# Row sums in the last column of the normalised operand, sweep 5's support step behind the next row's combination, x by blocks on SP's queue

## What is computed

```python
# layer 0
u = tanh([x, t] @ W1 + b1) @ W2 + b2
x = layernorm(x + u + adj @ (x @ B.T) - sum(adj, axis=1) * (x @ B.T))
# layer 1 (Chebyshev, three products with adj)
T1 = adj @ x; T2 = 2 * (adj @ T1) - x; T3 = 2 * (adj @ T2) - T1
x = layernorm(x + x @ w0 + T1 @ w1 + T2 @ w2 + T3 @ w3 + bias)
# layer 2
h = (adj @ x + x) / clip(sum(adj, axis=1) + 1, 1)
z = relu([x, h] @ W + b); x = layernorm(x + z / max(norm(z), 1e-12))
# layer 3
support = x @ weight
w = 0.5 ** (number of later nonzeros of the row), the last 100 only
x = layernorm(x + (adj != 0) * w @ support + bias)
```

## Time and profile before

| | |
|---|---|
| median of 3 runs | 3405.94 us (3402.93 to 3409.38) |
| the profiled execution, its own time | 3407.66 us |
| its span, first to last instruction | 3405.7 us |
| mean granted TensorE clock | 0.962 of full speed |
| PE busy | 3226.4 us (95%) |
| DVE busy | 3068.7 us (90%) |
| ACT busy | 2328.3 us (68%) |
| moved by DMA | 1150.26 MB, 338 GB/s |

### The profile page before, as it was taken

One profiled execution on the slowest core, in us unless ns is written; L12 is line 12 of the kernel. 1 busy time (PEld: TensorE's weight loads), 2 busy tenths in 40 slices (PEclk: granted clock), 3 DMA queues, 4 the chain that ended last, 5 costly groups with the idle time before them and its releaser, 6 DMA issues.

```text
span 3405.7 us, 37111 instructions
## 1 busy us (share of the span) xinstructions
PE 3226.4 (95%) x14316; PEld 2388.4 (70%) x14316; DVE 3068.7 (90%) x2614; ACT 2328.3 (68%) x1561; POOL 16.3 (0%) x39
## 2 busy tenths in 40 slices
PE   6999899999989999999998999988989999999998
PEld 5877677777767888778886788766767555555554
DVE  6778888999999988999889999988899899999997
ACT  4666456555467766877777766755566688888886
POOL 1000000000000000000000000000000000000000
PEclk9999999999999999999999999978888999999999
DMA  9888577677679999999999999967789999999996
GB/s 334 316 309 312 210 286 294 245 275 270 243 286 370 398 374 377 390 390 387 378 377 374 360 376 370 383 258 286 289 347 354 371 363 384 384 387 386 387 387 241
DMA packets 159837, 1150.26 MB, mean 338 GB/s; under 512 B 17968, under 2 KB 18160, under 8 KB 20336
## 3 DMA queue, kind: packets, MB, share of 16 engines
q1 hardware_dynamic: 156672, 1140.92, 86.5%
q0 software_dynamic: 544, 2.66, 0.4%
q10 hardware_dynamic: 2448, 4.33, 0.4%
HBM read 1145.74 MB, written 2.10 MB: 337 GB/s over the span
## 4 chain that ended last, share of the span: by engine, by line
PE 66%; DVE 27%; DMA 3%; issue 2%; ACT 2%; ACTq 0%; DVEq 0%
PE ACC L801 25%; DVE lo L562 16%; PE ACC L817 14%; PE ACC L926 13%; DVE GS L556 4%; PE PSF L940 3%; PE PST L940 3%; DMA raw<-in_at 2%; ACT hi L399 1%; PE PSF L890 1%; PE PSF L891 1%; PE PSF L883 1%; DVE SV L668 1%; PE PST L831 1%; PE PST L857 1%
## 5 line engine op out<-in xcount | busy, mean ns | idle before, releaser
L399 ACT CAST hi<-raw 128x2048 fp32r<-128x2048 f32 x832 | 1586.0, 1913 | 828.1 <-PE ACC L801 610.9
L562 DVE TENSOR_TENSOR lo<-raw,hi 128x2048 fp32r<-128x2048 f32 x832 | 1883.3, 2288 | 182.7 <-ACT hi L399 175.6
L801 PE MATMUL ACC<-hi,T 128*128 128x512 f32 x5568 | 1447.2, 398 | 33.5 <-POOL T L388 11.0
L801 PEld LDWEIGHTS ACC<-hi,T 128*128 128x128 f32 x5568 | 1060.2, 192 | 279.4 <-issue 45.8
L817 PE MATMUL ACC<-lo,T 128*128 128x512 f32 x3200 | 892.1, 401 | 100.9 <-DVE lo L562 99.6
L817 PEld LDWEIGHTS ACC<-lo,T 128*128 128x128 f32 x3200 | 606.9, 192 | 270.2 <-DVE lo L562 144.9
L405 ACT ACTIVATE Wf<-ACC,w_bias 128x1024 fp32r<-128x1024 f32 x512 | 569.2, 1115 | 138.3 <-PE ACC L926 138.1
L577 DVE SCALAR_TENSOR_TENSOR M<-raw,M 128x512 bf16<-128x512 f32 x1008 | 629.7, 685 | 36.3 <-PE ACC L926 23.7
L926 PE MATMUL ACC<-M,rank_b 128*128 128x512 bf16 x2032 | 528.9, 382 | 5.8 <-DVE M L577 2.1
L926 PEld LDWEIGHTS ACC<-M,rank_b 128*128 128x128 bf16 x2032 | 159.1, 98 | 264.2 <-issue 126.4
L940 PE MATMUL PST<-Wf,S 128*128 128x512 f32 x512 | 209.6, 490 | 0.0
(11 more groups left out here) (142 smaller groups left out, 1247.5 us busy)
## 6 DMA issues: line engine op xcount, KB each, us to landing
raw<-in_at SPq DMA_DIRECT2D x1088, 1024.0 KB, 6.0
O<-in_x_rows ACTq DMA_DIRECT2D x8, 256.0 KB, 35.7
SV<-in_x_cols POOLq DMA_DIRECT2D x1, 2048.0 KB, 27.9
out<-O ACTq DMA_DIRECT2D x8, 256.0 KB, 2.4
bias<-in_bias_rows ACTq DMA_DIRECT2D x1, 128.0 KB, 10.8
l1w_sb<-in_l_w POOLq DMA_DIRECT2D x2, 64.0 KB, 8.1
rank_f<-in_rank_mats POOLq DMA_DIRECT2D x1, 128.0 KB, 10.0
w_sb<-in_w POOLq DMA_DIRECT2D x2, 64.0 KB, 11.5
```

What stands on the lines that cost most here:

```text
L399: nc.scalar.copy(hi[:, c % NH], raw[:, c % NR]).then_inc(hi_done, 1)
L562: tt(lo[:, c % NR], raw[:, c % NR], hi[:, c % NH].bitcast(f32), ALU.subtract).then_inc(lo_done, 1)
L801: ins = mm(acc[:, part], w, hi[:, p.c % NH, s, part], start=opens and s == 0 and i == 0, stop=False)
```

## The change

Three things are changed.

1. **Row sums.** `write_v` leaves the last of the 64 columns of the normalised operand out (63 are written), so that column keeps the ones with which POOL filled it. A row of a layer norm sums to zero, so the missing column is minus the sum of the others, and the matrix `drop`, multiplied once at the start into `comb2` (`mix` on PE, `mixed` on DVE), puts it back where product 2 is used; where the operand itself is needed (`whole`, k = 3) it is kept in `RS`. `GS`, its adds, the matmuls with ones and `flush` are gone; `ut` takes all 128 partitions of both groups and adds them, and the accumulators alternate from group to group in sweep 1 as they do in the others.
2. **Sweep 5.** `l3w` is due behind pair c + 16 instead of c + 14, `s_hi` behind c + 20 instead of c + 17, `s_lo` behind c + 19 instead of c + 17. Layer 2's bias goes in as a 65th row of `comb`'s operands `TX` and `l2w_sb` instead of an add on DVE (line 632).
3. **x.** The blocks of x and `bias` are issued by SP, block b ahead of tile 4b, instead of by ACT all at the start.

The core of the diff:

```diff
-            if k == 1:
-                acc_of[k, kind, r] = 0 if kind == "P" or r == 0 else 1
-            else:
-                acc_of[k, kind, r] = turn % 2
-                turn += 1
+            acc_of[k, kind, r] = turn % 2
+            turn += 1
...
+    due("PE", 12, "mix", 1, 0)
+    due("DVE", 16, "mixed", 1, 0)
...
-            due("PE", c + 14, "l3w", k, r)
-            due("ACT", c + 17, "s_hi", k, r)
-            due("DVE", c + 17, "s_lo", k, r)
+            due("PE", c + 16, "l3w", k, r)
+            due("ACT", c + 20, "s_hi", k, r)
+            due("DVE", c + 19, "s_lo", k, r)
...
             for c in range(n_all):
+                if c < NB * NP and c % NP == 0:
+                    g = gs(pairs[c].J)
+                    sp.dma_start(O[:, g], x_rows[:, g]).then_inc(c_x[c // NP], 16)
+                    if c == 0:
+                        sp.dma_start(bias[:], bias_rows).then_inc(c_bias, 16)
...
                 dve.wait_ge(hi_done, c + 1)
-                for s in dve_sums(p):
-                    first = p.opens and s == 0
-                    if first:
-                        if p.r > 1:
-                            dve.wait_ge(gs_used, p.r - 1)
-                        link(copy(GS[:], raw[:, c % NR, s]))
-                    else:
-                        ins = tt(GS[:], GS[:], raw[:, c % NR, s], ALU.add)
...
                 dst = T[:, gs(I), :, 1 - u_slot(k)]
+                if k == 1:
+
+                    dst, src = dst[:, :, :, 0:D - 1], src[:, :, 0:D - 1]
...
-                    link(tt(xr[:], xr[:], over_rows(bias[:, 2, :]), ALU.add))
                     link(stt(sq[:], xr[:], 0.0, xr[:], ALU.max, ALU.mult))
...
-                    dve.wait_ge(ut_act, act_ut["ut" if r < 3 else "early", k, r])
+                    dve.wait_ge(ut_act, act_ut["ut", k, r])
+                    if kind == "P":
+                        dve.wait_ge(sv_act, act_sv["keep", k, r])
                     dve.wait_ge(pair_done, group_end[k, kind, r] + 1)
-                    tt(UT[u, :], UT[u, :], ACC[acc_of[k, kind, r]][u, :], ALU.add).then_inc(ut_dve, 1)
+                    tt(UT[:], UT[:], ACC[acc_of[k, kind, r]][:], ALU.add).then_inc(ut_dve, 1)
...
-                    if s in pe_sums(p):
-                        for h in range(2):
-                            part = slice(h * HALF, (h + 1) * HALF)
-                            ins = mm(sums[:, part], ones_st[:], hi[:, p.c % NH, s, part],
-                                     start=first_sum, stop=False)
```

More of the change, by code:

```diff
@@ L37, in graph_layers @@
 def graph_layers(nc, at, x_rows, x_cols, t_col, b_t, w1, w1_t, b1_c, w2, bias_rows, l1_w, l2_w, l3_w,
-                 ident, rank_mats, out):
+                 ident, rank_mats, drop, out):
     f32, f32r, bf16 = mybir.dt.float32, mybir.dt.float32r, mybir.dt.bfloat16
@@ L85, in graph_layers @@
     OT, _ = place("OT", [P, BLK], f32, UT_at)
-    GS, GS_at = place("GS", [P, BLK], f32)
-    ST = [place(f"ST{b}", [P, Q, 2, D], f32r, byte)[0] for b, byte in enumerate((UT_at, GS_at))]
-    TX, _ = place("TX", [D, BLK], f32, GS_at)
+    ST1, GS_at = place("ST1", [P, Q, 2, D], f32r)
+    ST = [place("ST0", [P, Q, 2, D], f32r, UT_at)[0], ST1]
+    TX, _ = place("TX", [D + 1, BLK], f32, GS_at)
     hT, hT_at = place("hT", [P, HC, BLK], f32)
@@ L200, in graph_layers @@
     due("DVE", 8, "consts", 1, 0)
+    due("PE", 12, "mix", 1, 0)
+    due("DVE", 16, "mixed", 1, 0)
+    due("DVE", group_end[4, "D", 1], "one", 4, 0)
     for b in range(1, NB):
@@ L215, in graph_layers @@
             due("ACT", c + 3, "diag", k, r)
-        if k == 1 and kind == "P" and r >= 3:
-            due("ACT", c + 3, "early", k, r)
-            due("PE", c + 2, "flush", k, r)
+        if k == 1 and c != row_end[k, r]:
+            due("ACT", c + 3, "ut", k, r)
+            if kind == "P":
+                due("ACT", c + 3, "keep", k, r)
         if c != row_end[k, r]:
@@ L221, in graph_layers @@
         if k == 1:
-            due("ACT", c + 2, "ut", k, r)
-            if r:
+            if r == 0:
+                due("ACT", c + 2, "ut", k, r)
+            else:
                 due("DVE", c + 2, "ut", k, r)
-            if 0 < r < 3:
+            if kind == "P":
                 due("ACT", c + 2, "keep", k, r)
@@ L684, in step @@
                         link(ins)
+                        link(copy(xo[:, :, D - 1], RS[:, g]))
                 elif what == "fin_a":
@@ L694, in step @@
                     nc.vector.reciprocal(RD[:, g], RD[:, g])
+                    copy(RS[:, g], xr[:, :, D - 1])
                     dve.wait_ge(w_done, r + 1)
@@ L775, in multiply @@
                 acc = ACC[acc_of[key]]
-                sums = ACC[1]
                 g = p.J * Q + 2 * p.pr
@@ L986, in lay_out @@
     later = np.tril(np.ones((P, P), np.float32), -1) - 256 * np.eye(P, dtype=np.float32)
+    drop = np.eye(D, dtype=np.float32)
+    drop[D - 1] -= 1
+    drop[D - 1, D - 1] = drop[:, D - 1] = 0
     return {
@@ L1005, in lay_out @@
         "rank_mats": c(np.stack([later, 1 - later], 1)),
+        "drop": c(np.tile(drop, (1, 2))),
     }
```

122 lines of the change are left out of this document (46 added, 76 removed).

## The result

The changed kernel takes 3225.25 us (median of 4 runs, 3221.74 to 3228.79), the kernel before took 3405.11 on the same chip (4 runs, 3402.93 to 3409.38): a ratio of 0.947, 95% interval 0.9454 to 0.9487.

The account below looks back on a forecast made before the run. The chain of waits was two thirds PE, with sweep 1's P groups held by DVE's adds into `GS`. 3407.7 - 113 (sweep 1) - 18 (sweep 5) + 0 (x) = 3276.7, less 1.7 for the median: 3275 us, range 3245 to 3310.

Parts of the forecast that it names:

- the 721 us of pairs and row steps: Sweep 1 from pair 32: 224 pairs at PE's 2.72 us, 609, plus seven rows' steps at 16.0, 112.
- 28 us were charged: Sweep 1: clock loss of 4 us for each of seven combinations, between nothing and the old 35.
- wrong if the clock fell in the P groups without a wait of PE: Sweep 1: sign against the prediction, the granted clock falling in P groups although PE isn't waiting; no size given.
- the one that carried row 0's combination over: Sweep 5, rows 1 to 3: 16.43 us from `l3w` to the next pair, less row 0's 8.07, makes 8.36 earlier.
- The order of the support step: Sweep 5: later `l3w`, `s_hi`, `s_lo` save 5.9 us in each of rows 0 to 2, 18; later rows 0.
- x by blocks: Start and sweep 1's first row: gains and delays sum to 0, between 4 us less and 20 more.
- DVE wait for block 2 behind the fifth tile: Start: block 2 lands some three tiles, 8 us, after the fifth tile; PE's supply covers part, half the gain is lost.
- the 33 foreseen: Start: sign in the changed kernel's profile, the fifth tile at about 33 us.
- New waits at row ends: Rival, sweep 1: `ut` waits for ACT's copies and `comb` for it, 72 us over seven rows, 3347; chance 0.05.
- openings of accumulators that wait: Rival, slower kernel: sweep 1's 14 accumulator openings each wait 10.3 us, 144 in all, 3419; chance 0.02.
- The support step that only moves its wait: Rival, sweep 5: `s_hi` and `s_lo` hold `fin_b`, losing the combination's gain; price 18 us, 3293; chance 0.07.
- x late: Rival, sweep 1's first row: late blocks of x hold it up; price 20 us, 3295; chance 0.08.

Follow-up runs that it names:

- e7: Changed kernel with the 168 copies and adds of sweep 1's P groups back on DVE, into a buffer nobody reads: 3332.24 us.
- e8: Changed kernel with 224 matmuls with weights of zero back on PE in sweep 1's P groups: 3269.88 us.
- e12: e1 with each 128-row matmul of the combination overwriting the 64-row product instead of adding to it, same alternating order: 3255.28 us.
- e6: Changed kernel with only the row sums kept: 64-row combination, support step at its old place, x issued by ACT: 3271.44 us.
- e1: Changed kernel with sweep 5's combination back to 64 rows and layer 2's bias added on DVE, new order kept: 3258.57 us.
- e9: Changed kernel with x in rows and bias issued by ACT all at the start, as before: 3226.31 us.
- e3: e1 with the eight 64-row matmuls first, then the eight 128-row ones, which overwrite instead of adding: 3228.86 us.
- e4: Changed kernel with the support step back at its old place, 65 rows kept: 3243.96 us.
- e10: Changed kernel with each block of x in rows issued four tiles earlier by SP: 3224.12 us.
- e11: e10 with x in columns also sent in eight blocks over SP instead of one 2 MB transfer on POOL's queue: 3209.41 us.

## Why the forecast fell short

**Sweep 1: the mechanism was right, one term was off.** PE sets the pace in every group, and the 721 us of pairs and row steps hold. The term that was mis-sized is the clock: 28 us were charged, four for each of seven combinations. The clock fell in two of the seven, at about 5 us each, so 10 us: 721 + 3 + 10 = 734, measured 731.9. The charge lay near its upper bound, the 35 us that the kernel before lost in a stretch where PE waits. e7 and e8 show how much goes with such waits: 0.06 x 844.6 = 51 us were lost with them, 0.01 x 782.6 = 8 without (the rounded clock allows 4 to 12). The 5.0 us that S1 lost in the earlier trace rows were one such fall, in row 0's combination; in the changed kernel S1 had none. The forecast also said that it would be wrong if the clock fell in the P groups without a wait of PE. It did, in P3 and P5, where the combinations of rows 2 and 4 lie; that was in the sum, only too highly priced.

**Sweep 5: the step that failed** is the one that carried row 0's combination over: "In row 0 nothing stands ahead, and a combination takes 2241.15 - 2233.08 = 8.07", with the new row costed only as DVE's add of 0.7 us. The edit changed the combination itself, from 8.07 us to 3.5. By the four corners the 65th row gives 24 to 28 of the 49 us. The Trainium skill's rule on drains, quoted under e12, should have stood among the rivals as the one on the gaining side. That something cost here could be seen: in the earlier trace rows 16 matmuls took 8.07 us, while `l3w`'s matmuls of 64 rows, half as many of fewer columns, took 2.00. I read 8.07 as a price of matmuls and did not ask why they were twice as dear as their neighbours. It held turns, 2.7 us, and a fall of the clock inside it: its first parts took 0.78 us and its last 1.34.

**The order of the support step** was forecast at 18 us, 5.9 for each of rows 0 to 2, and this term was right. With the 64 rows for which it was worked out, from the start of row 0's combination to that of row 3's it is 2253.07 - 2101.07 = 152.0 us in e6 and 2238.04 - 2104.72 = 133.3 in e1: 18.7, or 6.2 a row. There `s_lo` waited 1.05, 2.19 and 1.25 us, where 1.8 was estimated. The other 4 of the 23 us lie in the rows behind, which were put at 0: in e6 the clock fell inside the combinations of rows 4 and 5 (8.2 and 8.3 us) and in e1 it did not (6.3 and 6.6). The wait of PE for `lo` behind `l3w` is there (5.76, before 4.50), as is the combination without a wait ahead of it.

**Part of both gains is clock.** Sweep 5's granted clock rose from 0.85 to 0.94. 0.15 x 474.0 - 0.06 x 424.8 = 46 us of lost clock time came back, nearly as much as the stretch gained. Not all of it can have been on the path, since PE's waits for `lo` rose from 43.3 us to 57.6 in the same stretch. The views don't divide it further: a wait that goes, a turn that goes and a clock that stays up are one event in each row.

**x by blocks** was put at 0 and is 0 (e9 against the changed kernel: 1.1 us, within what can be told). The sum was right, the reasons only half: I let DVE wait for block 2 behind the fifth tile and for one or two us; it waited for block 1, ahead of the second `lo`, for 18.09. That cost nothing because the fifth tile would have been late anyway: with ACT issuing x, e9's comes at 34.58 us, having waited 12.88 for its tile, and its pair 32 starts within 1 us of the same time. The fifth tile's `hi` at 34.17 us looks like the 33 foreseen, but what held it was DVE.

**The last stretch** gained 7 us that the forecast did not have. The eighth row's combination lies in it, shorter by 8.3 - 3.7 = 4.6 us. The kernels with 65 rows take 734.6 to 737.1 us for the stretch (nine of them), those with 64 rows in turns 737.4 to 741.4 (before, e1, e6, e12), which fits; but the two groups all but touch, and e3 takes 737.9 with a short combination. No run took this row alone, and the cause stays open.

**The rivals.** New waits at row ends, and openings of accumulators that wait, did not appear: PE is busy in all of sweep 1, and e6 has the same 732.6. The support step that only moves its wait is refuted by e4. x late did happen in the mechanism and not in the time. None of the rivals stood for a faster kernel than the forecast: no mechanism on the gaining side was priced beyond the bounds of the terms, and there 50 us lay.

## What to carry to other kernels

When an edit changes the shape of an operation, its price is a term of its own, even if only one row is added: compare the old price first with neighbours of the same kind, and a matmul that costs twice its neighbours is a finding to chase before the forecast. Charge the clock by what PE does in the new kernel and not by what was lost in the old one: where the waits go, their clock loss goes with them. What stays are the falls without a wait, here two or three in seven combinations, 5 us each, and they also set how small a difference between two traces means anything. And take off a busy engine's load only after asking what lay beside it: here the adds were worth 113 us and the matmuls 51 when put back singly, against 133.5 together.

## What the runs showed of the hardware

- Single-precision matmuls of 64 rows and of 128 rows in turn cost 0.78 us a pair at full clock, 1.34 at the lower of the two clock levels (granted 0.50); 65 rows and 128 in turn 0.45 and 0.85 to 0.88; 64 rows among themselves and 128 among themselves together 3.78 us for eight pairs, 0.47 each. It makes no difference whether the second adds to the first or overwrites it (e12).
- In e12 the clock fell inside a combination of such turns without any wait of PE shown (a 64-row matmul took 0.48 us before and 0.79 after), and in none of the 65-row combinations that began at full clock.
- In sweep 1 the clock fell to 0.50 inside two or three of seven combinations of a row although PE was busy throughout (10.2 to 11.3 us for a combination against 7.3), at other rows in other kernels; the stretch took 731.9 to 732.6 us with two falls and 735.8 to 737.5 with three.
- In sweep 1 the granted clock was 0.94 with gaps between PE's matmuls and 0.99 with 224 more matmuls and no gap.
- One 2 MB transfer on another queue set when the fifth 1 MB tile was usable: its `hi` came at 35.38 us with it (e10) and at 24.13 without (e11).
